# Attending x in blocks of 8 rows and 16 pixels instead of 4 rows and 32, with GpSimd laying the blocks out

## What is computed

```python
k = conv(x, w1, rhs_dilation=(2, 2), padding=6) + b1        # 256 -> 128 channels, 7x7
k = conv(k, w2) + b2                                        # 128 -> 49, 1x1
attn = softmax(k, axis=1)                                   # 49 weights of a pixel
shifts = [xp[:, :, 2*u:2*u+H, 2*v:2*v+W] for u in range(7) for v in range(7)]
x = einsum('bkchw,bkhw->bchw', stack(shifts), attn)         # the part that the change touches
y = gelu(yc.T[None, :, None, :] + x * D)                    # yc: states of a scan, one column vector per w
o = x + y
out = (o - mean_c(o)) * rsqrt(var_c(o) + eps) * ln_w + ln_b
```

## Time and profile before

| | |
|---|---|
| median of three runs | 814.69 us (812.89 to 814.72) |
| the profiled execution | 813.03 us, span 810.9 us, granted TensorE clock 0.983 |
| PE, ACT, DVE, POOL busy | 758.2, 566.1, 677.6, 191.0 us |
| one unit in the steady state | 89.8 us (from logits of one unit to logits of the next, 390.64 to 480.44 us) |
| matmuls recorded | 12,242 |

### The profile page before, as it was taken

The page is one execution under the profiler, slowest core; times in us unless marked ns, Lnnn a source line. Parts: engine busy times, 40 slices in busy tenths (PEclk is TensorE's granted clock), DMA queues, the critical chain, the costliest instruction groups (busy, mean ns, idle before and its releaser), DMA issues.

```text
span 810.9 us, 27182 instructions
## 1 busy us (share of the span) xinstructions
PE 758.2 (93%) x12242; PEld 448.2 (55%) x12242; DVE 677.6 (84%) x867; ACT 566.1 (70%) x917; POOL 191.0 (24%) x102
## 2 busy tenths in 40 slices
PE   4969989999999999999999999999999999997994
PEld 1535545764567545664567545764567455754671
DVE  0898997989888988989888888998888888595765
ACT  2873545768786796678786787678786777568546
POOL 4114113114211341114301431115302421022011
PEclk9979999999999999999999999999999999999988
DMA  9460050001602035201702053201711020201104
GB/s 295 130 105 2 3 93 16 3 1 24 135 4 53 3 77 81 55 2 27 132 2 55 2 107 53 55 2 27 132 27 30 2 53 4 55 2 48 39 22 104
DMA packets 133598, 41.78 MB, mean 52 GB/s; under 512 B 133145, under 2 KB 133226, under 8 KB 133226
## 3 DMA queue, kind: packets, MB, share of 16 engines
q1 hardware_dynamic: 132248, 40.01, 22.2%
q10 hardware_dynamic: 1234, 0.04, 0.1%
HBM read 23.27 MB, written 16.78 MB: 49 GB/s over the span
## 4 chain that ended last, share of the span: by engine, by line
PE 42%; ACT 20%; DVE 17%; issue 5%; POOL 2%; DVEq 0%; ACTq 0%
PE cv L484 20%; PE wk L525 9%; PE wk L544 4%; ACT chs L903 4%; ACT V L860 4%; PE wk L583 3%; POOL chs L371 2%; PE ms L556 2%; DVE o L1507 2%; DVE V L1359 2%; DVE Z L1400 2%; ACT ms L953 1%; DVE XT L1390 1%; DVE chs L1459 1%; DVE o L1520 1%
## 5 line engine op out<-in xcount | busy, mean ns | idle before, releaser
L484 PE MATMUL cv<-V,W 128*32 128x496 f16 (+6 forms) x7840 | 428.2, 374 | 3.6 <-issue 1.9
L484 PEld LDWEIGHTS cv<-V,W 128*32 128x32 f16 (+1 forms) x7840 | 198.8, 96 | 201.4 <-issue 15.3
L860 ACT ACTIVATE V<-R,sc 128x1024 f16<-128x1024 f32 (+1 forms) x88 | 109.6, 1274 | 59.6 <-DVE R L1285 50.7
L346 POOL TENSOR_TENSOR R<-raw 128x1152 f32<-128x1152 f32 x32 | 93.1, 2909 | 205.6 <-DVE V L1359 102.8
L1359 DVE SCALAR_TENSOR_TENSOR V<-R,sc,V 128x1024 f16<-128x1024 f32 (+1 forms) x88 | 115.1, 1328 | 2.6 <-ACT V L860 2.6
L544 PE MATMUL wk<-band,XT 128*128 128x224 f16 (+1 forms) x900 | 97.3, 266 | 0.9
L544 PEld LDWEIGHTS wk<-band,XT 128*128 128x128 f16 x900 | 76.6, 98 | 24.6 <-ACT o L926 6.0
L525 PEld LDWEIGHTS wk<-AT,sel 128*128 128x128 f16 x2368 | 73.5, 100 | 15.0 <-issue 11.0
L525 PE MATMUL wk<-AT,sel 128*128 128x16 f16 x2368 | 77.8, 193 | 0.1
L371 POOL TENSOR_TENSOR chs<-o 128x1024 f32<-128x1024 f32 x14 | 45.1, 3223 | 132.1 <-DVE o L1507 123.1
L1285 DVE SCALAR_TENSOR_TENSOR R<-R 128x1024 f32<-128x1024 f32 (+1 forms) x56 | 70.3, 1287 | 0.0
(11 more groups left out here) (194 smaller groups left out, 916.9 us busy)
## 6 DMA issues: line engine op xcount, KB each, us to landing
raw<-in_x_dram SPq DMA_DIRECT2D x16, 1024.0 KB, 11.3
out_dram<-o SPq DMA_DIRECT2D x28, 512.0 KB, 4.5
w1raw<-in_L_conv_w_dram SPq DMA_DIRECT2D x2, 3136.0 KB, 16.8
out_dram<-o SPq DMA_DIRECT2D x8, 256.0 KB, 3.9
cm<-in_L_conv_Cmat_dram ACTq DMA_DIRECT2D x1, 32.0 KB, 8.3
dcol<-in_L_conv_D_dram ACTq DMA_DIRECT2D x2, 0.5 KB, 10.2
lnw<-in_L_conv_ln_w_dram ACTq DMA_DIRECT2D x2, 0.5 KB, 7.3
lnb<-in_L_conv_ln_b_dram ACTq DMA_DIRECT2D x2, 0.5 KB, 7.4
```

The costliest lines, as they stand in the source:

```text
L346: nc.gpsimd.tensor_tensor(R[buffer][:, :, :, :], rows_of(par, j + 2), rows_of(par, j), ALU.subtract).then_inc(pool_rows, 1)
L484: ins = pe.matmul(to.rearrange("p (w t c) -> p w t c", w=2, c=COLS)[:, :, :, c0:c1], W[:, ws, h * K7 + v, k0:k1], slot(n, a)[:, low, :, t0 ...
L860: nc.scalar.activation(v_array(n, a, 0), array(a), ACT.Identity, scale=sc[:, par, 3:4]).then_inc(vhi, 1)
```

## The change

A block of x is now 8 rows by 16 columns (128 pixels again). It reaches 14 rows and 19 columns: the 16 of its own and the 3 beyond it on the one side that is not the image's edge. The band has 8 blocks of 14 rows of 2 x 19 columns. The transposes need the 128 pixels of a block in one row, so GpSimd copies them out of raw first (`tile_rows`, L414 of the changed kernel), two copies of 2 x 8 x 16 pixels for each of the eight groups, into a ring of three buffers: the inner rows of the two halves of `AT`, and a new `xs`.

```diff
+            def tile_rows(n, par, g):
+                k = STAGES * n + g
+                if g >= 3:
+                    pool.wait_ge(xt_done, k - 2)
+                elif n:
+                    pool.wait_ge(sel_done, STEPS * n)
+                    pool.wait_ge(xt_done, STAGES * n)
+                if n:
+                    pool.wait_ge(raw_in[par], 16 * n + (16 if par else 0))
+                j, e = TROWS * (g // XTILES) + PAD, 2 * TCOLS * (g % XTILES)
+                for w in range(2):
+                    nc.gpsimd.tensor_copy(stage(k)[:, w], raw[par][:, :, j:j + TROWS, e + w:e + 2 * TCOLS:2]).then_inc(xs_in[k % 3], 1)
@@ GpSimd, a unit
+                tile_rows(n, par, 0)
+                tile_rows(n, par, 1)
+                tile_rows(n, par, 2)
                 sum_rows(m, 0)
+                tile_rows(n, par, 3)
+                tile_rows(n, par, 4)
                 sum_squares(m, 0)
+                tile_rows(n, par, 5)
                 sum_rows(m, 1)
+                tile_rows(n, par, 6)
                 if nxt:
                     make_c0(n + 1, 1 - par)
+                tile_rows(n, par, 7)
                 sum_squares(m, 1)
@@ GpSimd, the start
-            nc.gpsimd.memset(AT[:].rearrange("p w r c -> p (w r c)").bitcast(U32), 0).then_inc(late_cleared, 1)
+            for r in (0, PAD + ROWS):
+                nc.gpsimd.memset(AT[:, :, r:r + PAD, :].rearrange("p w r c -> p w (r c)"), 0.0).then_inc(late_cleared, 1)
+            tile_rows(0, 0, 0)
+            tile_rows(0, 0, 1)
+            tile_rows(0, 0, 2)
             make_w(0, 0)
+            tile_rows(0, 0, 3)
+            tile_rows(0, 0, 4)
             pool.wait_ge(s_border, 4)
             make_c1(1, 1)
+            tile_rows(0, 0, 5)
+            tile_rows(0, 0, 6)
             amax(1, 1)
+            tile_rows(0, 0, 7)
             make_c0(1, 1)
@@ TensorE, spread
-                for c in range(COLS):
-                    s = c + 1 if c < PAD else c - COLS + 7 if c >= COLS - PAD else 0
-                    f = (BROWS - 1 - r) * COLS + COLS - 1 - c
-                    ins = pe.matmul(spread_bank(m, r)[:, c * TILES:(c + 1) * TILES].rearrange("p (w j) -> p w j", w=2),
-                                    sel[:, s, f:f + P],
-                                    AT[:, :, r:r + 29:4, c], start=True, stop=True)
+                for k, (c, edge) in enumerate(SPREAD[r]):
+                    v = 3 - c if c < PAD else c - 6 if c > TCOLS - PAD - 1 else 0
+                    for row in range(BROWS):
...
+                        ins = pe.matmul(to, sel[:, f:f + P], attention, start=True, stop=True)
@@ TensorE, apply
-                for j in range(ROWS // 4):
-                    r0, r1 = max(4 * j - PAD, 16 * q), min(4 * j + 4 + PAD, 16 * q + 16)
+                for j in range(XROWS):
+                    r0, r1 = max(TROWS * j - PAD, 16 * q), min(TROWS * j + TROWS + PAD, 16 * q + 16)
                     if r0 >= r1:
                         continue
...
+                    for e in range(XTILES):
+                        to = out_rows[:, r0 - 16 * q:r1 - 16 * q, (COLS - BCOLS) * e:(COLS - BCOLS) * e + BCOLS]
...
@@ TensorE, turn_x
-                        rows = raw[par][:, h, PAD + 4 * j:PAD + 4 * j + 4, :].rearrange("p r w -> p (r w)")
-                        ins = pe.transpose(wk[:, g % 2, c:c + P], rows[:, w:4 * WIDTH:2], id32[:, :])
+                        ins = pe.transpose(wk[:, g % 2, c:c + P], stage(k)[:, w, h].rearrange("p r c -> p (r c)"),
+                                           id32[:, :])
@@ TensorE, the start
-            turn_x(0, 0, 0, cold=True)
-            turn_x(0, 0, 1, cold=True)
             bias_products()
             conv(0, 0, 6, cold=True)
+            turn_x(0, 0, 0, cold=True)
+            conv(0, 6, 10, cold=True)
+            turn_x(0, 0, 1, cold=True)
+            conv(0, 10, 16, cold=True)
             turn_x(0, 0, 2, cold=True)
-            conv(0, 6, 14, cold=True)
+            conv(0, 16, 26, cold=True)
             turn_x(0, 0, 3, cold=True)
-            conv(0, 14, 30, cold=True)
+            conv(0, 26, 30, cold=True)
```

More of the change, by code:

```diff
@@ L33 @@
 LN_EPS = 1e-5
-SEL_TAPS = ((0, 7), (3, 7), (2, 7), (1, 7), (0, 6), (0, 5), (0, 4))
-SEL_AT = PAD * COLS + COLS - 1 - PAD
+SEL_TAPS = ((0, 7),) + tuple((v, 7) for v in range(1, 7)) + tuple((0, v) for v in range(6, 0, -1))
+SEL_AT = K7 * TCOLS + TCOLS - 1
+SEL_STEP = SEL_AT + (K7 - 1) * TCOLS + K7
+SEL_WIDTH = (len(SEL_TAPS) - 1) * SEL_STEP + 2 * SEL_AT + (K7 - 1) * TCOLS + K7
+SEL_DONE = 2 * len(SEL_TAPS) + 1
+SPREAD = tuple(((c, None), (c + 1, None)) for c in range(0, TCOLS, 2))
+SPREAD += (((16, 0), (17, 0), (18, 0), (-3, 1)), ((-2, 1), (-1, 1)))
+STEPS = len(SPREAD)
 ATT_SCALE = 4096.0
@@ L194, in conv_seq_kernel @@
         raw = (raw0, raw1)
+        stages = [AT[:, w, PAD:PAD + ROWS, :].rearrange("p r c -> p (r c)").bitcast(F32) for w in range(2)] + [xs[:, :]]
+        stage = lambda k: stages[k % 3].rearrange("p (w h r c) -> p w h r c", w=2, h=HALVES, r=TROWS)
         ms = ctx.enter_context(nc.psum_tensor("ms", [P, 2, BANK], F32))
@@ L202, in conv_seq_kernel, with band_step @@
         last_banks = [wk[:, 0, :], wk[:, 1, :]] + [cv[:, i, :] for i in range(4)]
+        spread_out = lambda m, s: spread_bank(m, s)[:, 0:2 * XROWS * BROWS * 4].rearrange(
+            "p (n e c) -> p n e c", e=2, c=2)
+        edge_out = lambda m, s: spread_bank(m, s)[:, 0:2 * XROWS * BROWS * len(SPREAD[s])].rearrange(
+            "p (n c) -> p n c", c=len(SPREAD[s]))
+        def band_step(low, s):
+            rows = band[:, low].rearrange("p n r x -> p (n r) x")
+            if s < TCOLS // 2:
+                return rows.rearrange("p n (y z) -> p n y z", z=2)[:, :, s:s + 12:11, :]
+            first = TCOLS if s == TCOLS // 2 else TCOLS + len(SPREAD[s - 1])
+            return rows[:, :, first:first + len(SPREAD[s])]
+        sum_of_step = lambda m, s: (spread_out if s < TCOLS // 2 else edge_out)(m, s)
         spread_bank = lambda m, r: last_banks[r % 6] if m == LAST else wk[:, r % 2, :]
@@ L699, in keep_warm @@
                     pe.wait_ge(s_pcopy, CHUNKS * HALVES * GROUPS)
-                    pe.wait_ge(s_sel, 15)
+                    pe.wait_ge(s_sel, SEL_DONE)
                 for _ in range(IDLE_AT_START[k]):
-                    pe.matmul(pprod[:, 0, 0:14 * COLS], id16[:, :], sel[:, 0, :], start=True, stop=True)
+                    pe.matmul(pprod[:, 0, 0:14 * COLS], id16[:, :], sel[:, 0:14 * COLS], start=True, stop=True)
             def scan_outputs():
@@ L805, in _ @@
             keep_running(2)
-            for r in range(BROWS):
+            for r in range(STEPS):
                 spread(m, r)
@@ L916, in band_high @@
                 act.wait_ge(sel_done, 10 * m + r + 1)
[L917 to L918 removed]
+                nc.scalar.copy(band_step(0, r), sum_of_step(m, r)).then_inc(bhi, 1)
             def attended(m, par, y):
@@ L1228, in _ @@
             scale_shift(m - 1, 1, 1)
-            for r in range(4, BROWS):
+            for r in range(4, STEPS):
                 band_high(m, r)
```

72 lines of the change are left out of this document (43 added, 29 removed).

## The result

| | before | after |
|---|---|---|
| median of 20 runs | 812.86 us (812.19 to 814.94) | 815.18 us (812.04 to 818.04) |
| ratio | | 1.0022, 95% interval 1.0013 to 1.0031 |
| profiled execution, span | 813.03, 810.9 us | 816.11, 814.2 us |
| POOL, DVE, PE busy | 191.0, 677.6, 758.2 us | 290.4, 684.9, 746.2 us |

A forecast was written before the change was run, and what follows sets the result against it. TensorE bounds mean(m, 1) to apply; the layer-norm chain equally bounds apply to mean and mean to mean. Unit 0 +7.7, six units +6.0, unit 7 -0.5, last -1.4: +11.8, 824.8 us (+10 against the median); range 811 to 834.

The forecast's parts named there:

- The stretch from 812.2 to 817.1: Whole-kernel time interval in the chances, described as part of the short copies case: chance 0.15.
- Copy cost: GpSimd's copies of 256 float32 a partition: 0.42 us each back to back, bounds 0.28 and 0.68.
- That a plain copy takes the lock: GpSimd copies and VectorE instructions with two SBUF inputs lock each other out for a whole instruction.
- Mean to mean: Steady unit, between the means: three copies come first on a VectorE without gaps, TensorE waits 1.26 us longer.
- Apply to mean: Steady unit: six copies, 2.5 us, against VectorE gaps of 2.36; residual(0, 0) 0.1 us later, apply's 0.4 gain lost.
- 0.032 each whatever their columns: Steady unit's spread: matmuls take 0.032 us each at any width; twelve fewer save 0.38 us.
- Unit 0: First unit: +7.7 us, from 4.2 at group 0's transpose, 2.7 for copies of groups 3 to 6, 0.8 for group 7.
- copies of groups 3 to 6: Unit 0: eight copies meet a VectorE without air, four fifths on two-SBUF-input work: 8 x 0.42 x 0.8 = 2.7 us.
- Last unit: Last unit: spread saves 0.38 us and apply 1.0, together -1.4 us.
- the lock costs nothing: Rival: copies leave VectorE alone or fall into its gaps; unit 0 +4.2, a unit -0.8, 810 us; chance 0.17.
- Short copies: Rival: copies take 0.28 us; unit 0 +6.6, six units 0, last two -2.2, 817.4 us; chance 0.2.
- Scattered writes: Rival: spread's 16 single columns written apart slow matmuls, say 50 ns each: +44, 869 us; chance 0.03.

The follow-up runs named there:

- second pair of profiles: The kernel before and the changed kernel, each profiled once more without edits: spans 812.8 and 811.6 us.
- early copies: Changed kernel, but in unit 0 GpSimd does its clears and copies of groups 0 to 2 before make_c2, not behind it: 808.83 us, 0.9945 of before.
- kernel without copies: The kernel with early copies, with no copies in units 1 to 7 (every transpose reads xs, x not laid out rightly): 805.83 us, 0.9888 of before.
- copies beside centre: The kernel with early copies, but GpSimd copies groups 3 and 4 only when VectorE is through with logits_rows: 807.52 us, 0.9914 of before.

## Why the prediction was right or wrong

*Direction and place*: slower, and most of it by unit 0: right, but narrowly, as the second pair of profiles has it the other way. The size, +10 against +2.3 us between the medians, was wrong, because units 1 to 6 did not lose 6.0 us but gained 1.7. The stretch from 812.2 to 817.1, where the result lies, had 0.15.

*Copy cost*, 0.42 us: near enough (0.36 back to back, 0.40 alone). *That a plain copy takes the lock*: right. The Trainium skill's rule ("SBUF — State Buffer", Who interferes with whom) says who meets whom, and the trace agrees on both sides: logits_rows with two SBUF inputs is lengthened, centre with one is not. It calls the shared ports an exclusive lock, and I took from it and from rows 5 and 7 that the second waits for the whole of the first; the rows show 0.24 us for a copy that lasts 0.40.

*Mean to mean, +1.26 us*: this step failed. It took three copies at their full length, "three copies come first". Measured: two contacts of 0.24, one for each logits_rows; +0.43 in all. Both factors were wrong: the number is that of the VectorE operations with two SBUF inputs that are met, and the price is less than the copy's duration. The earlier trace rows showed only whole long operations waited for, from which neither can be read.

*Apply to mean, +0.1 and the 0.4 of apply lost*: failed in the same way. Six copies were 2.5 us against gaps of 2.36; in fact the first two lengthened one VectorE operation each (1.41 to 1.57 and 1.21 to 1.44 us), and four fell into VectorE's idle 1.5 us. x1_plus, the row sum that the rows of before have at 431.55, itself took 1.74 us instead of 2.08 in this profile and 2.26 with early copies, and mean(m, 0) came as early in both. The kernel without copies has the same mean(m, 0) to 0.02 us. So the gains ahead of it arrived: 0.47 us before apply starts (0.38 forecast) and two y at 0.15 each (0.2 forecast), 0.76 together. "0.032 each whatever their columns" was not quite so: from start to start the spread matmuls of 16 columns take 0.033 us, those of 8 columns 0.027. The -0.8 a unit that I gave for copies that cost nothing is what the kernel without copies and with copies beside centre shows (-0.9 and -0.8). For six units the two steps are 6 x 1.3 = 7.8 us of the error, nearly all of it.

*Unit 0, +7.7*: 9.5 in the profiled pair; from the convolution's start 8.8 (73.5 against 64.8), and 5.9 in the second pair of profiles (71.2 against 65.3), where v_low was ahead of make_c0 in the changed kernel but not in the kernel before (with the 2.4 us of that in both, 8.3). The stand was 3.83 us (3.3 forecast). The half clock, 2.6 us, had no term. In exchange the copies of groups 3 to 6, 2.7 us forecast, met VectorE at few places: 0.87, 0.59 and 0.98 us for operations of 0.68, 0.45 and 0.75 at 102 to 104.6 us, 0.6 in all. The total was near the truth because two errors cancelled, which is luck.

*Last unit, -1.4*: mis-sized, for a reason outside the sum. VectorE's pace for one y went from 1.52 to 1.37 us, 0.9 over six, and the forecast had 1.0. The other two microseconds go with the clock: where the kernel before ran ten microseconds at half speed, the changed one did not. Why it did not is open. Windows of the last unit before, and then after:

```profile
768.00:777.00 9.00, 8.56 (x158) 6.25 (x155) 4.08 (x7) 5.01 (x8) 0.00 (x0) 0.50 0.41 105
```

```profile
769.00:780.00 11.00, 10.91 (x317) 9.87 (x316) 7.08 (x13) 8.36 (x14) 0.00 (x0) 1.00 0.43 98
```

*Rivals*: "the lock costs nothing" missed unit 0 (4.2 us, 9.5 measured), 2.6 us of it by the half clock and not by the lock; for the steady units it gave -0.8, where -0.3 was measured with the copies and -0.9 without. "Short copies" gives 817.4, nearest to the result, for the wrong reason: the copies aren't short, their contacts are. Scattered writes: the spread's matmuls of 16 columns take 0.033 us each against 0.032; excluded. The Trainium skill's rule on non-contiguous patterns ("PSUM — Partial Sum Buffer", Specifications) is not borne out at this size: the measurement decides.
